# One decoder layer on one core: projection pieces, statistics a batch ahead, and the first unit and feed-forward prologue in another order

## The reference

```python
x = x + attn(layernorm(x))      # 16 heads of 128; slots of 64 per head: exp(s), cumulated, softmax over slots, rope
x = x + xattn(layernorm(x), ctx, mask, mask)   # 16 heads of 16, over 8 batches, keys from ctx
x = x + ffn(layernorm(x))       # silu(x w1') * (x w2') w3', weights through a 4-bit round trip
```

```python
q = Wq @ target + bq; k = Wk @ source + bk; v = Wv @ source + bv      # 256 x 512 per batch
dot = mask * (q.k / 4) - (1 - mask) * 1e6
out = softmax(dot) * mask @ v                                         # per head, 512 x 512
```

## Time and profile before

| what | value |
|---|---|
| time, median of 3 runs | 2219.49 us (2218.57 to 2231.32) |
| the profiled execution's own time, its span | 2217.53 us, 2215.5 us |
| mean granted TensorE clock | 0.982 |
| PE busy | 2105.6 us (95%), 11638 matmuls |
| DVE, ACT, POOL busy | 1559.6 (70%), 803.9 (36%), 762.4 (34%) |
| costliest DVE group, x_mx (L1712) | 512 reductions, 683 ns each |
| last chain: PE, issue | 10%, 1% of the span followed |

### The profile page before, as it was taken

How to read it: one execution, slowest core, us unless ns; L and a number is a source line. 1 busy time by engine, 2 the same in 40 slices (tenths; PEclk the granted TensorE clock), 3 DMA queues, 4 the chain that set the end, 5 groups by cost and what they waited for, 6 DMA issues and landing times. The chain is left out here.

```text
span 2215.5 us, 35363 instructions
## 1 busy us (share of the span) xinstructions
PE 2105.6 (95%) x11638; PEld 1499.3 (68%) x11638; DVE 1559.6 (70%) x2829; ACT 803.9 (36%) x1843; POOL 762.4 (34%) x532
## 2 busy tenths in 40 slices
PE   5899999999999999999999999889999999699998
PEld 4677787887887778878878878643333333278776
DVE  7657887887887556878878888568888887432221
ACT  1223233233233232332332332317667766652221
POOL 3234344344343343443443433321222221221211
PEclk9999999999999999999999999989999999999999
DMA  6121011011111220110101110474566654311110
GB/s 214 38 95 56 8 54 44 24 54 30 38 54 36 77 106 2 55 45 24 54 32 37 54 34 4 82 153 90 104 118 119 119 103 92 113 38 58 58 38 20
DMA packets 60484, 142.36 MB, mean 64 GB/s; under 512 B 10942, under 2 KB 25478, under 8 KB 55398
## 3 DMA queue, kind: packets, MB, share of 16 engines
q1 hardware_dynamic: 57622, 138.65, 24.0%
q10 hardware_dynamic: 2768, 2.51, 0.5%
HBM read 93.47 MB, written 17.54 MB: 50 GB/s over the span
## 5 line engine op out<-in xcount | busy, mean ns | idle before, releaser
L1712 DVE TENSOR_REDUCE x_mx<-x_pm 128x1 f32<-128x512 f32 x512 | 324.0, 683 | 58.3 <-PE x_pm L1814 57.5
L1553 ACT ACTIVATE x_E<-x_pd 128x512 f32<-128x512 f32 x497 | 266.7, 602 | 117.9 <-PE x_pd L1833 116.9
L1140 PE MATMUL a_pj<-a_wvg_h,q_big 128*128 128x512 f32 x1024 | 287.0, 408 | 4.2 <-DVE a_rm L800 4.2
L1124 PE MATMUL a_pj<-q_big,a_wqk_h 128*128 128x512 f32 x1024 | 290.1, 405 | 0.4 <-POOL a_wqk_l L632 0.4
L1140 PEld LDWEIGHTS a_pj<-a_wvg_h,q_big 128*128 128x128 f32 x1024 | 186.1, 189 | 54.1 <-issue 4.8
L1124 PEld LDWEIGHTS a_pj<-q_big,a_wqk_h 128*128 128x128 f32 x1024 | 183.1, 188 | 40.0 <-POOL a_wqk_l L632 1.3
L800 DVE TENSOR_TENSOR a_rm<-a_pj,a_rope 128x1024 f32<-128x1024 f32 x128 | 155.5, 1216 | 74.1 <-PE a_pj L1124 72.8
L519 ACT ACTIVATE a_v<-a_pj 128x256 f32<-128x256 f32 x128 | 49.1, 384 | 420.3 <-PE a_pj L1140 420.3
L670 POOL TENSOR_TENSOR a_ogl<-a_ogf,a_ogh 128x512 fp32r<-128x512 f32 x62 | 82.2, 1347 | 282.0 <-ACT a_ogf L558 282.0
L892 DVE TENSOR_TENSOR a_acc<-a_po,a_acc 128x512 f32<-128x512 f32 x128 | 85.9, 687 | 88.3 <-PE a_po L1253 88.3
L1847 PE MATMUL x_pa<-x_E,x_vx 128*32 128x512 f32 x1024 | 140.7, 612 | 1.0 <-ACT x_raw L1567 1.0
(11 more groups left out here) (228 smaller groups left out, 4503.9 us busy)
## 6 DMA issues: line engine op xcount, KB each, us to landing
a_qk_raw<-in_wqk SPq DMA_DIRECT2D x16, 1024.0 KB, 5.4
a_vg_raw<-in_wvg SPq DMA_DIRECT2D x16, 1024.0 KB, 4.9
a_wo_raw<-in_wo SPq DMA_DIRECT2D x16, 512.0 KB, 3.6
x_Q<-x_hi SPq DMA_DIRECT2D x20, 256.0 KB
x_K<-x_hi SPq DMA_DIRECT2D x20, 256.0 KB
a_acc<-in_w SPq DMA_DIRECT2D x6, 704.0 KB, 4.3
a_wt<-in_w SPq DMA_DIRECT2D x24, 176.0 KB, 2.3
weights_scratch<-a_wt SPq DMA_DIRECT2D x24, 176.0 KB, 1.9
```

Source lines behind the costliest of these rows:

```text
L1124: last = mm(pj[:, j % 2, :], wa[:, c, j * P:(j + 1) * P], xa[:, c, p * UT:(p + 1) * UT], start=k == 0, stop=k == 11)
L1140: last = mm(pj[:, tt % 2, :], xa[:, c, t0:t0 + P], wa[:, c, :], start=k == 0, stop=k == 11)
L1553: nc.scalar.activation(E[:, n % ESLOTS, :], dot_bank(n), ACT.Exp, scale=XD ** -0.5).then_inc(exp_done, 1)
L1712: nc.vector.reduce_max(mx[:, u % 2, at:at + 1], pm[:, k % 3, :], AX_X).then_inc(pm_done, 1)
```

## The change

In the self-attention, the mask's first products run on VectorE ahead of the first variances; the three high copies and three scaled rows move from VectorE to ScalarE (behind the first weight split); the two low rows stay on VectorE, ahead of the first scores. In the first unit `project_vg` 1 and 2 come ahead of `scores` 0 and 1, and the gate products follow that order. In the cross-attention a projection is cut into four pieces of 256 columns and one channel half each; the table PIECES spreads the 24 pieces over steps 1 to 15, query first; fills, context load, x load, store, `norm_stats` and `norm` move with it. In the feed-forward prologue the last four takes of VectorE alternate with the four bn_stats.

```diff
             sp.wait_ge(rows_b, 6)
+            sp.wait_ge(rows_l, 2)
...
+            def mask_highs():
+                act.wait_ge(rows_a, 2)
+                for row, src in ((0, ra), (2, rb), (3, rb)):
+                    nc.scalar.activation(mq[row].bitcast(F32R), src, ACT.Copy).then_inc(rows_h, 1)
+                act.wait_ge(rows_h, 3)
+                act.wait_ge(rows_l, 1)
+                for row, src in ((2, 0), (3, 1), (4, 0)):
+                    nc.scalar.activation(mk[row].bitcast(F32R), mq[src], ACT.Copy, scale=-4.0).then_inc(rows_b, 1)
...
             high_qk(0)
+            mask_highs()
...
+            def mask_lows():
+                dve.wait_ge(rows_h, 3)
+                nc.vector.tensor_tensor(mq[1].bitcast(F32R), ra, mq[0], ALU.subtract).then_inc(rows_l, 1)
+                nc.vector.tensor_tensor(mq[4].bitcast(F32R), rb, mq[2], ALU.subtract).then_inc(rows_l, 1)
...
                 rotate(n, 0)
-                if isinstance(n, int) and n == 0:
-                    mask_products(0)
...
                 rotate(n, 1)
-                if isinstance(n, int) and n == 0:
-                    mask_products(1)
...
                 rotate(n, 2)
-                if isinstance(n, int) and n == 0:
-                    mask_products(2)
...
+                if not began(n, 1):
+                    gate_product(n, p, 1)
                 a_evac(n, 0)
                 a_evac(n, 1)
                 if began(n, 1):
                     gated(m, pm)
-                gate_product(n, p, 1)
+                    gate_product(n, p, 1)
+                else:
+                    gate_product(n, p, 2)
...
+            mask_products()
             variances(0)
             normalised(0)
             low_x(0)
+            mask_lows()
             scores_in(0)
...
-                scores(n, 0)
-                project_vg(n, g, p, 1)
-                scores(n, 1)
-                project_vg(n, g, p, 2)
+                if began(n, 1):
+                    scores(n, 0)
+                    project_vg(n, g, p, 1)
+                    scores(n, 1)
+                    project_vg(n, g, p, 2)
+                else:
+                    project_vg(n, g, p, 1)
+                    scores(n, 0)
+                    project_vg(n, g, p, 2)
+                    scores(n, 1)
...
-            return (2, 3, 0, 1, 4, 5) if b > 1 else (0, 1, 2, 3, 4, 5)
+            return (0, 1, 2, 3, 4, 5)
...
-        FILLS = {9: ((1, 0),), 10: ((1, 1),), 11: ((1, 4),), 12: ((1, 5),), 13: ((1, 2),), 14: ((1, 3),)}
-        LATE = {k + 1: ((0, k),) for k in range(6)}
+        PIECES = {1: (0, 2), 2: (0, 2), 3: (1, 1), 4: (1, 2), 5: (1, 1), 6: (2, 2), 7: (2, 2), 8: (3, 1), 9: (3, 2), 10: (3, 1),
+                  11: (4, 1), 12: (4, 2), 13: (4, 1), 14: (5, 2), 15: (5, 2)}
+        TAKEN = {2: 0, 5: 1, 7: 2, 10: 3, 13: 4, 15: 5}
+        FILLS = {7: ((0, 0),), 8: ((0, 1),), 9: ((0, 2),), 10: ((0, 3),), 11: ((0, 4),), 12: ((0, 5),),
+                 13: ((1, 0),), 14: ((1, 1),), 15: ((1, 4),)}
+        LATE = {0: ((1, 5),), 1: ((1, 2),), 2: ((1, 3),)}
...
-                    if b and G in (5, 13):
-                        store(2 * b - 2 + (G == 13))
+                    if b and G in (5, 10):
+                        store(2 * b - 2 + (G == 10))
...
-                        if G == 0:
+                        if G == 1:
                             load_c(b + 2)
...
-                    if G == 15 and b + 3 < B:
+                    if G == 12 and b + 3 < B:
                         load_x(b + 3)
...
-                    if G in (6, 8, 10, 12) and t // 4 + 2 < B:
-                        high(t // 4 + 2, order(2)[G // 2 - 3])
+                    if TAKEN.get(G - 1, 4) < 4 and t // 4 + 2 < B:
+                        high(t // 4 + 2, TAKEN[G - 1])
...
+            norm_stats(2, 0)
+            norm_stats(2, 1)
             for t in range(QUADS):
...
+                    if G == 0 and b + 2 < B:
+                        norm(b + 2, 0)
+                        norm(b + 2, 1)
+                    if G in TAKEN and b + 2 < B:
+                        take_projection(b + 2, TAKEN[G])
                     if u < QUADS:
                         row_max(u, q, (2, 3))
...
-                        if G == 4:
-                            norm_stats(b + 2, 0)
-                            norm_stats(b + 2, 1)
-                        if G == 6:
-                            norm(b + 2, 0)
-                            norm(b + 2, 1)
+                    if G == 14 and b + 3 < B:
+                        norm_stats(b + 3, 0)
+                        norm_stats(b + 3, 1)
...
-                    if G >= 4 and b + 2 < B:
-                        project_part(b + 2, order(2)[G // 2 - 2], G % 2)
+                    if G in PIECES and b + 2 < B:
+                        j, n = PIECES[G]
+                        first = sum(m for g, (i, m) in PIECES.items() if i == j and g < G)
+                        for k in range(first, first + n):
+                            project_part(b + 2, j, k)
...
                 for tt in range(4):
-                    if first and tt == 2:
-                        dve.wait_ge(x_in, 16)
+                    if first:
+                        if tt % 2 == 0:
+                            dve.wait_ge((x_first, x_in)[tt // 2], 16)
+                        take(BY_DVE - 4 + tt)
                     V.bn_stats(stats[:, tt, :], xt[:, tt, :]).then_inc(stat, 1)
...
-            for r in range(BY_DVE - 2):
+            for r in range(BY_DVE - 4):
                 take(r)
             norm_stats(0)
-            for r in range(BY_DVE - 2, BY_DVE):
-                take(r)
```

More of the change, by code:

```diff
@@ L719, in _, with mask_products @@
         def _(dve):
[L720 removed]
+            def mask_products():
                 V = nc.vector
[L723 to L737 removed]
                 dve.wait_ge(m_in, 16)
@@ L1641, in _ @@
             values(1, 1)
+            rsqrt(2)
             clear(pool, spent)
@@ L1646, in _ @@
                 if b + 2 < B:
-                    rsqrt(b + 2)
-                if b + 2 < B:
-                    for j in order(2)[0:3]:
-                        low(b + 2, j)
+                    low(b + 2, 0)
+                    low(b + 2, 1)
                 if b:
@@ L1760, in _ @@
                         max_rows(u - 1)
-                    if G in range(5, 16, 2) and b + 2 < B:
-                        take_projection(b + 2, order(2)[G // 2 - 2])
+                    if G == 0 and b + 2 < B:
[3 more added lines that the diff above has]
+                        take_projection(b + 2, TAKEN[G])
                     if u < QUADS:
@@ L1789, in project_part @@
                     after(pe, pp_done, projected(b, j) - (b < 2))
-                dst = bank(b, j)
+                h, c = k // 2, k % 2
+                dst, q = bank(b, j)[:, 0, 256 * h:256 * h + 256], 2 * (j - 4) + h
                 if j < 4:
                     w, src = ((wq_t, xn), (wk_t, cx))[j // 2]
-                    last = mm(dst[:, 0, :], w[:, k, (j % 2) * P:(j % 2 + 1) * P], src[:, k, :], start=k == 0, stop=k == 1)
+                    last = mm(dst, w[:, c, (j % 2) * P:(j % 2 + 1) * P], src[:, c, 256 * h:256 * h + 256], start=c == 0, stop=c == 1)
                 else:
-                    q = 2 * (j - 4) + k
-                    for c in range(2):
-                        last = mm(dst[:, 0, k * 256:(k + 1) * 256], cx[:, c, q * P:(q + 1) * P], wv_t[:, c, :],
-                                  start=c == 0, stop=c == 1)
-                if k:
+                    last = mm(dst, cx[:, c, q * P:(q + 1) * P], wv_t[:, c, :], start=c == 0, stop=c == 1)
+                if k == 3:
                     last.then_inc(pp_ready, 1)
             def project(b, j):
-                project_part(b, j, 0)
-                project_part(b, j, 1)
+                for k in range(4):
+                    project_part(b, j, k)
             def row_scores(u, q, i):
@@ L2033, in _, with take @@
             V = nc.vector
+            def take(r):
+                dve.wait_ge(w12_ready, 2 * r + 2)
+                V.tensor_copy(w2[:, :, r * P:(r + 1) * P], spread(turned(1, r))).then_inc(taken_dve, 1)
             def norm_stats(g):
                 first = isinstance(g, int) and g == 0
-                if first:
-                    dve.wait_ge(x_first, 16)
-                else:
+                if not first:
                     dve.wait_ge(x_in, 16 * g + 16)
@@ L2098, in step @@
                     add(g, tt)
-            def take(r):
-                dve.wait_ge(w12_ready, 2 * r + 2)
-                V.tensor_copy(w2[:, :, r * P:(r + 1) * P], spread(turned(1, r))).then_inc(taken_dve, 1)
-            for r in range(BY_DVE - 2):
+            for r in range(BY_DVE - 4):
                 take(r)
             norm_stats(0)
-            for r in range(BY_DVE - 2, BY_DVE):
-                take(r)
             normed(0, 0)
```

30 lines of the change are left out of this document (9 added, 21 removed).

## The result

The changed kernel takes 2244.40 us (median of 6 runs, 2234.49 to 2248.56) against 2224.60 us before (6 runs, 2218.57 to 2231.32): a ratio of 1.008 (the means of the runs give 1.0082, the medians 1.0089), 95% interval 1.0058 to 1.0103. I had forecast 2200.6 us, range 2191 to 2212. The profiled execution takes 2239.05 us with a span of 2236.5, against 2217.53 and 2215.5; the mean granted clock fell from 0.982 to 0.973 of full speed.

What follows compares the result with a forecast made beforehand. TensorE was read as busy nearly everywhere, each stage judged by its own stretches. The terms -8.4, -7.0, -10.1, +1.6, +3.5, +1.5 sum to -18.9 us: 2198.6 for the profiled execution, 2200.6 against the median, range 2191 to 2212.

Steps and rivals of the forecast that it cites:

- First unit, -8.4: Self-attention's first unit: earlier rotations and projections ahead of scores save 8.4 us, 0.5 for mask products at the head included.
- x one batch ahead, +3.5: Cross-attention, step 14: `norm_stats` waits for the mask half of `load_x`, 0.7 us in five batches, 3.5 us lost.
- Rival C: Cross-attention: `norm_stats` waits for the slowest mask landing, 10.2 us, and the clock falls; 2230 us, slower by 10; chance 0.04.
- Pieces, -7.0: Cross-attention: projection pieces over fifteen steps, one-piece steps at 2.97 us, gain 1.17 us in each of six batches, 7.0.
- rival B: Cross-attention: half the gain, as one-piece steps cost 3.17 us or landings are 6.8; 2207 to 2213 us; chance 0.18.
- Context and fills, -10.1: Cross-attention: earlier context load and fills remove waits, 5.7 us in batches 1, 5 and 2, 4.4 in batch 6.
- Statistics and norm, +1.6: Cross-attention: moved statistics and `norm` cost 1.6 us net, 2.2 of it for batch 2's block ahead of the loop.
- Feed-forward prologue, +1.5: Feed-forward start: seven takes instead of five before the aggregation make normalised x 1.6 to 2.4 us late, 1.5 us lost.
- Rival D: Cross-attention: 96 extra weight loads stand exposed, 18 us eat the gain; 2219 us; chance 0.02.

Runs made afterwards that it cites:

- e4: The kernel before with only the change's first-unit part (mask rows, projection order, gate products); 2217.73 us, ratio 0.9951.
- e1: The changed kernel with the load of x and its mask issued at step 11, ahead of the fills, instead of step 12; 2210.51 us, ratio 0.993.
- e3: e1 with the statistics of batch 2 moved from behind the start's last projection to among the projections taken of batch 1; 2206.87 us, ratio 0.9915.
- e5: e1 with the projections again in twelve steps, two pieces in each of steps 4 to 15; 2213.10 us, ratio 0.9925.
- e8: e1 with batch 0 in the old order and the next batch's statistics split over steps 13 and 14; 2215.18 us, ratio 0.9943.
- e10: The changed kernel with the load of x and mask still in step 12, but ahead of its copies and fills; 2209.05 us, ratio 0.992.
- e7: e3 with the feed-forward prologue's copies and statistics in the order of the kernel before; 2207.09 us, ratio 0.9909.
- e9: e5 with statistics at steps 0 and 1, norm at step 3, the old feed-forward prologue and GpSimd's `rsqrt` first; 2211.36 us, ratio 0.9924.

## Why the prediction was wrong, point by point

The span grew by 21.0 us: 8.0 gained ahead of the cross-attention, 14.4 lost at its start, 27.5 lost to the late load, some 13.2 gained elsewhere in its quads (the remainder), 0.3 lost behind it.

- **First unit, -8.4: right.** 8.0 in the changed kernel, 9.2 in e4, and the places named (34.7, 41.9, 56) were 34.25, 41.63 and 55.01. At the head VectorE waits for the mask until 2.97 and its statistics begin at 4.82 instead of 4.50, 0.3 of the 0.5 charged; nothing of it lasts, TensorE's first product into `a_mid` starts at 15.49 instead of 15.89. The figure that the prediction cites there from the Trainium skill (DMA: Bandwidth & Descriptors, "Anatomy of one DMA") is fitted on transfers issued by GpSimd; the mask comes from ScalarE's queue and took at most 2.2 us (0.76 to 2.97), near the 2.0 of that figure. What the sum lacked is the next stage's context load: e4 lost 4.3 us at it, in a trace where it landed 1.8 us later.
- **x one batch ahead, +3.5: this is the step that failed.** The transfer's side was right: 11.0 us from the quad's start to the mask's landing forecast, 1602.4 - 1591.2 = 11.2 measured. VectorE's side was not: I had it at `norm_stats` after 10.3 us, and it is there after 1599.95 - 1591.21 = 8.7 (8.6 in e1). So the wait is 2.3 to 3.1 us instead of 0.7. And I charged a microsecond for each one waited, although and the earlier trace rows hold a stretch that lost 4.4 for a wait of 3.12, with its clock at 0.95; the runs give two on average, one for the wait and one for the clock behind it. 5 x 0.7 became 12.9 x 2.1 = 27. Why VectorE is there 1.6 us earlier than I had it, no run isolates.
- **Rival C, chance 0.04, is what happened**, by its mechanism if not by its number: not a landing of 10.2 us (it was 6.0), but a VectorE 1.6 us earlier. I had tied C to the landing alone, the one side for which the trace spoke against it. C's price with the clock was +29; the term measured 27.5. That they are so near is luck: C has waits 4.5 us longer than forecast, at 5.8 each with the clock; the real ones are 1.9 us longer (2.6 instead of 0.7) and cost 5.5.
- **Pieces, -7.0: wrong in the sum, right in its premise.** A one-piece step does take 2.96 to 2.97 us (three of six, e3). But the sum let all six take that, and left every two-piece step at 3.39. Per batch, e3 against e5: steps 1 to 3 cost 0.98 more, as forecast; the five other one-piece steps gain 1.35 instead of 2.1; and steps 4, 6 and 14 cost 0.60 more. That makes +0.2 instead of -1.17. The loss in step 6 is rival B's mechanism, VectorE's take behind four maxima; I had argued it away with the 0.2 us that three banks carry.
- **Context and fills, -10.1: right.** Batch 1's pair became shorter by 4.75 us, batch 6's by 4.59, and batch 5's by 0.93; batch 2's lies under the late load.
- **Statistics and norm, +1.6: right in the steady batches, wrong at the start.** In the undisturbed quads the statistics cost 14.57 - 13.70 = 0.87 (e5), up to 14.55 - 13.57 = 0.98 (e3, seven pieces), and `norm` in the shortest step nothing that shows (12.50 in e5, 12.51 before). For batch 2 I took 2.2 us from the earlier trace rows; the start lost 14.4, of which the context's late landing may be 6 (a first stretch of some 24.5 us at a wait of 4.3, between e4 and e8 in the table) and three steps' pieces 1. In the rest, some 7, VectorE is full, statistics there stop TensorE (1.51 us at 1489.50) and the clock goes with it (0.50 from 1494 to 1498): the same factor left out a second time. No run separates the shares further.
- **Feed-forward prologue, +1.5: right in place, open in size.** The first `f_pt` comes 1.7 us later (1.6 to 2.4 forecast), and the end 0.3 us later in this pair of traces, some 1 over all.
- **Rival D** (weight loads) stays without support: eight pieces of 256 columns make 13.70 us in e5, and the four half projections of a quad before made 13.70.

Had only the late load been right, 2239.05 - 27.5 = 2211.6 would have been the profiled time; e1 and e10 measured ratios of 0.993 and 0.992, that is 2207 to 2209 against the median of 2224.6 before. From 2211.6 to the 2198.6 forecast for that execution 13.0 are left: the pieces' 7.0 and the start's 14.4 - 2.2 = 12.2 are more than that, and against them stand the 3.5 charged for x and some 2.7 that came out better elsewhere.

## What to carry to other kernels

When a load is moved nearer to its first reader, compute both arrivals from the same start, and price the wait by a stretch of the same trace that already has one, with its clock: here each microsecond of VectorE's wait cost two on average, one where the clock stayed up and up to 3.5 where it did not. Then look at what stands ahead of the load in its own queue, since 3 to 6 us of order within one step were 27.5 us of this kernel. And when work is spread by steps, look at the step behind the lightened one, and at the other engines' work in it: VectorE's take moved the gain into a loss one step on. Every version with the load in time beats both kernels; the lowest ratios are those of e7, e3 and e10 (0.9909, 0.9915 and 0.992, not told apart by their intervals), and e10 is the changed kernel with two lines moved.

## What the runs showed of the hardware that was not expected

- TensorE's clock after a stop. In the changed kernel a stop of 2.86 us was followed by a granted clock of 0.50 from about 1605 to 1615, with TensorE busy for 10.00 of 10.00 us in it; until 1604.5, nearly the whole stop, it was still 1.00. Two stops of 2.73 us were followed by some 3 us at 0.50, one of 1.84 us (e9) and one of 1.39 (e1) by some 7 us, one of 1.13 (e8) by none.
- `norm`, a VectorE instruction from and to on-chip memory, took 2.88, 2.02 and 2.70 us for its two halves in three batches of e9, each time while GpSimd made its sums, and 0.99 to 1.00 in the others. In one of those, batch 2, GpSimd's sum began 0.7 us behind `norm`, and there the sum was the longer one: 1.46 us instead of 1.28. By the Trainium skill (SBUF — State Buffer, "Who interferes with whom") VectorE and GpSimd share a pair of ports that one instruction holds for its whole length, and `tensor_scalar` is among those that can take it. The trace agrees: `norm`'s 2.88 us end at 1553.46, after the second of GpSimd's sums (1551.84 + 1.33 = 1553.17) and not after its own length.
- The same 512 KB context load of batch 1 landed after 7.5, 7.7, 9.1, 9.3, 9.4, 9.8, 10.9, 11.5, 11.5, 12.4, 12.5 and 12.7 us in twelve kernels that issue it at the same place. A schedule that needs it after 7.5 is late in most of them.
